# The attention output is turned by VectorE in 32x32 blocks instead of by TensorE, and the PSUM ring is laid out anew

## The reference

```python
# layer 0: softmax attention, 16 heads of 32
xn = layer_norm(x);  q, k, v = xn @ Wq + bq, xn @ Wk + bk, (xn @ Wv + bv) * mask
y  = softmax(q @ k.T + mask_bias, axis=keys) @ v            # per head
h  = layer_norm(y) * (1 + scale(emb)) + shift(emb)
x1 = x + silu(h) @ W_out0 + b_out0
# layer 1: linear attention, 8 heads of 64
xn = layer_norm(x1); q = softmax(xn @ Wq1 + bq1, axis=head features)
k  = softmax(xn @ Wk1 + bk1 + mask_bias, axis=positions);  v = (xn @ Wv1 + bv1) * mask
y  = q @ (k.T @ v)                                          # per head
out = x1 + silu(layer_norm(y) * (1 + scale) + shift) @ W_out1 + b_out1
```

## Time and profile before

| what | value |
|---|---|
| median of 3 runs | 2692.48 us (2691.06 to 2693.92) |
| profiled execution | 2693.01 us |
| its span, first to last instruction | 2691.2 us |
| mean granted TensorE clock | 0.992 |
| busy: TensorE, VectorE, ScalarE, GpSimd | 2629.1, 1793.8, 1250.1, 1348.6 us |
| first instruction of the second phase's turns | 1475.5 us into the span |

### The profile page before, as it was taken

One profiled execution on the slowest core, in us unless ns is written; L12 is line 12 of the kernel. 1 busy time (PEld: TensorE's weight loads), 2 busy tenths in 40 slices (PEclk: granted clock), 3 DMA queues, 4 the chain that ended last, 5 costly groups with the idle time before them and its releaser, 6 DMA issues. The chain is left out here.

```text
span 2691.2 us, 44011 instructions
## 1 busy us (share of the span) xinstructions
PE 2629.1 (98%) x13890; PEld 1938.4 (72%) x13890; DVE 1793.8 (67%) x3213; ACT 1250.1 (46%) x2097; POOL 1348.6 (50%) x634
## 2 busy tenths in 40 slices
PE   7999999999999999999998899999999999999999
PEld 5666666666666666666663688888888888888887
DVE  6666666666666666666664876776666776766765
ACT  3555555555565555555554333323333333333233
POOL 1666666666666666666662234334443333344343
PEclk9999999999999999999998899999999999999999
DMA  6666666666566665666674301111111111011110
GB/s 146 99 86 106 101 100 85 106 100 100 85 102 99 99 99 84 104 101 100 85 138 151 127 28 42 45 47 51 51 51 51 51 47 42 33 51 35 49 33 32
DMA packets 114916, 211.44 MB, mean 79 GB/s; under 512 B 12409, under 2 KB 14509, under 8 KB 114877
## 3 DMA queue, kind: packets, MB, share of 16 engines
q1 hardware_dynamic: 78012, 143.81, 22.9%
q10 hardware_dynamic: 36864, 67.13, 18.9%
HBM read 74.87 MB, written 34.18 MB: 41 GB/s over the span
## 5 line engine op out<-in xcount | busy, mean ns | idle before, releaser
L942 DVE TENSOR_REDUCE negmax<-max_bank 128x1 f32<-128x512 f32 x1024 | 681.8, 688 | 259.5 <-PE max_bank L535 256.6
L806 ACT ACTIVATE probs<-exp_bank 128x512 f32<-128x512 f32 x1024 | 586.9, 597 | 496.9 <-PE exp_bank L550 424.2
L297 POOL TENSOR_TENSOR probs_sum<-probs_sum,probs 128x2048 f32<-128x2048 f32 x124 | 571.6, 4610 | 31.1 <-ACT probs L806 24.4
L297 POOL TENSOR_TENSOR probs_sum<-probs 128x2048 f32<-128x2048 f32 x63 | 289.2, 4590 | 501.3 <-ACT probs L806 501.3
L550 PE MATMUL exp_bank<-q_stack,k_stack 100*128 100x512 f32 x1024 | 422.7, 422 | 2.9 <-ACT probs L806 2.0
L535 PE MATMUL max_bank<-k_stack,q_stack 98*128 98x512 f32 x1024 | 417.2, 408 | 4.7 <-DMA k_stack<-k_stage 2.3
L550 PEld LDWEIGHTS exp_bank<-q_stack,k_stack 100*128 100x128 f32 x1024 | 193.2, 189 | 127.9 <-ACT probs L806 45.8
L535 PEld LDWEIGHTS max_bank<-k_stack,q_stack 98*128 98x128 f32 x1024 | 192.8, 189 | 106.9 <-issue 54.3
L1601 POOL TENSOR_TENSOR sT_lo<-silu,sT_hi 128x512 fp32r<-128x512 f32 x124 | 167.6, 1371 | 173.2 <-DVE sT_hi L1719 173.2
L561 PE MATMUL y_bank<-probs,v_sb 128*32 128x512 f32 x2048 | 248.7, 604 | 0.0
L1346 PE MATMUL b_work<-ident,area 128*128 128x128 f32 x1536 | 190.7, 278 | 16.7 <-DVE area L1687 9.9
(11 more groups left out here) (209 smaller groups left out, 5329.3 us busy)
## 6 DMA issues: line engine op xcount, KB each, us to landing
q_stack<-q_stage ACTq DMA_DIRECT2D x128, 256.0 KB
k_stack<-k_stage ACTq DMA_DIRECT2D x128, 256.0 KB
x_sb<-in_x SPq DMA_DIRECT2D x16, 1024.0 KB, 5.3
q_stack<-q_stage SPq DMA_DIRECT2D x64, 256.0 KB
k_stack<-k_stage SPq DMA_DIRECT2D x64, 256.0 KB
yT_scratch<-y_stage SPq DMA_DIRECT2D x64, 256.0 KB
area<-yT_scratch SPq DMA_DIRECT2D x16, 1024.0 KB, 5.2
area<-in_x SPq DMA_DIRECT2D x64, 256.0 KB, 2.8
```

The lines of the kernel that those rows point to most:

```text
L297: eng.tensor_tensor(probs_sum[:, :, :], so_far, probs[:, mt, :, :], ALU.add).then_inc(probs_added, 1)
L806: act.activation(probs[:, mt, j, :], exp_bank[k % 2][:, :], ACT.Exp).then_inc(exp_done, 1)
L942: dve.tensor_reduce(negmax[:, m:m + 1], max_bank[m % 2][:, :], AXX, ALU.max, negate=True).then_inc(max_done, 1)
```

## The change

1. A is no longer done by TensorE. Its tiles leave the ring. VectorE turns each of its four tiles in 32x32 blocks from SBUF to SBUF (`turn_blocks`), then multiplies it by the reciprocals in place (`scale_heads`), then takes its statistics. TensorE still turns the sums (four small transposes).
2. So that 32x32 blocks are enough, the scratch has another layout: `store_y` writes 128 partitions x 4 runs of 512 B instead of 128 runs of 2 KB, ScalarE's `copy_y` permutes as it copies, and `load_y` is four DMAs of 32 partitions (256 KB each) instead of one of 1 MB. SyncE issues it when A's four block turns and the turn of the sums are done.
3. The four places that A leaves in the ring stay empty (`"-"`): two behind K's tiles and two between M and S. A place that nobody fills passes its wait on to the next tile in that bank.

```diff
-        ORDER = (tiles_of("KL") + [("V", 0), ("V", 1)] + tiles_of("A") + [("V", 2), ("V", 3)] + tiles_of("MSH")
+        ORDER = (tiles_of("K") + [("-", 0), ("-", 1)] + tiles_of("LVM") + [("-", 2), ("-", 3)] + tiles_of("SH")
                  + [("Q", 0), ("Q", 1)] + tiles_of("C") + [("Q", 2), ("Q", 3)] + tiles_of("JXY"))
...
-                sp.dma_start(yT_dram[b].rearrange("(j g l) t -> g j l t", j=HG, g=NG)[g], y_stage[:, g % 2, :]).then_inc(y_stored[g % 2], DMA)
+                sp.dma_start(yT_dram[b].rearrange("q j l g r -> g (j l) q r")[g],
+                             y_stage[:, g % 2, :].rearrange("p (q r) -> p q r", q=BLOCKS)).then_inc(y_stored[g % 2], DMA)
...
-                act.activation(y_stage[:, g % 2, :], y_bank[:, :], ACT.Copy).then_inc(y_read, 1)
+                act.activation(y_stage[:, g % 2, :].rearrange("p (q t a) -> p q t a", q=BLOCKS, t=TT),
+                               y_bank[:, :].rearrange("p (t q a) -> p q t a", t=TT, q=BLOCKS), ACT.Copy).then_inc(y_read, 1)
...
-                sp.dma_start(yT_sb, yT_dram[b].rearrange("(g p) t -> p g t", p=P)).then_inc(y_in, DMA)
-                sp.dma_start(sums_sb[:, :], sums_dram[b]).then_inc(y_in, DMA)
+                for q in range(BLOCKS):
+                    at = slice(q * BLOCK, (q + 1) * BLOCK)
+                    sp.dma_start(y_blocks[at, :].rearrange("l (j r) -> l j r", j=HG), yT_dram[b][q].rearrange("j l g r -> l j (g r)")
+                                 ).then_inc(y_in, DMA)
+                sp.dma_start(sums_sb[:, :], sums_dram[b]).then_inc(sums_in, DMA)
...
-                        sp.wait_ge(work_full, use(kind, b, "A", TT - 1)[1] + 1)
+                        sp.wait_ge(y_turned, TT * (b + 2))
+                        sp.wait_ge(sums_turned, b + 2)
                         load_y(b + 2)
...
-                V(kind, b, (0, 1))
+                V(kind, b, (0,))
+                if kind != "last":
+                    await_sums(b + 1)
+                V(kind, b, (1,))
...
-                    A(kind, b, b + 1)
+                    turn_sums()
                 V(kind, b, (2, 3))
```

More of the change, by code:

```diff
@@ L17 @@
+from collections import namedtuple
 from contextlib import ExitStack
@@ L1195, in order_of @@
         def order_of(kind):
+            if kind == "start":
+                return START
             if kind in ("last", "end"):
@@ L1198, in order_of, with counts @@
             return [u for u in ORDER if not (kind == "first" and u[0] in "LM")]
-        PER_ROW = len(ORDER)
-        assert PER_ROW % RING == 0
-        def use(kind, b, what, tile):
-            if kind == "start":
[L1206 to L1210, removed]
+        assert len(ORDER) % RING == 0
+        FIRST_AT = len(START)
+        ROW_AT = FIRST_AT + len(order_of("first")) - len(ORDER)
+        def counts(kind, at, tiles):
+            banks, full = [0] * RING, 0
+            for i, u in enumerate(order_of(kind)[:tiles]):
+                if u[0] != "-":
+                    banks[(at + i) % RING] += 1
+                    full += 1
+            return banks, full
+        START_READS, START_FULL = counts("start", 0, len(START))
+        FIRST_READS, FIRST_FULL = counts("first", FIRST_AT, len(ORDER))
+        ROW_READS, ROW_FULL = counts("mid", ROW_AT, len(ORDER))
+        Use = namedtuple("Use", "bank full reads")
+        def use(kind, b, what, tile):
+            order = order_of(kind)
+            n = order.index((f"end {what}" if kind == "end" else what, tile))
+            at = {"start": 0, "first": FIRST_AT}.get(kind, ROW_AT)
+            banks, full = counts(kind, at, n)
+            i = (at + n) % RING
+            if kind == "start":
+                return Use(i, full, banks[i])
+            full, reads = full + START_FULL, banks[i] + START_READS[i]
+            if kind == "first":
+                return Use(i, full, reads)
+            return Use(i, ROW_FULL * b + full + FIRST_FULL - ROW_FULL, ROW_READS[i] * b + reads + FIRST_READS[i] - ROW_READS[i])
         def bank(u):
-            return work_bank[u[0] % RING][:, :]
-        def reads(b, u):
-            return (PER_ROW // RING) * b + u[0] // RING
+            return work_bank[u.bank][:, :]
         def wait_read(eng, kind, b, what, tile):
             u = use(kind, b, what, tile)
-            eng.wait_ge(bank_read[u[0] % RING], reads(b, u) + 1)
+            eng.wait_ge(bank_read[u.bank], u.reads + 1)
         def wait_x1T(eng, kind, b):
@@ L1269, in _ @@
             load_weight("out1", out1_w)
-            sp.wait_ge(work_full, use("start", 0, "A", TT - 1)[1] + 1)
+            sp.wait_ge(y_turned, TT)
+            sp.wait_ge(sums_turned, 1)
             load_y(1)
@@ L1310, in take @@
                 u = use(kind, b, what, tile)
-                if u[0] >= RING:
-                    pe.wait_ge(bank_read[u[0] % RING], reads(b, u))
+                if not (type(u.reads) is int and u.reads == 0):
+                    pe.wait_ge(bank_read[u.bank], u.reads)
                 return bank(u)
@@ L1347, in turn, with await_sums, turn_sums @@
                 last.then_inc(work_full, 1)
-            def A(kind, b, row):
-                pe.wait_ge(y_in, 2 * DMA * (row + 1))
+            def await_sums(row):
+                pe.wait_ge(sums_in, DMA * (row + 1))
                 if not (type(row) is int and row == 0):
                     pe.wait_ge(rinv0_done, row)
[L1354 to L1360, removed]
+            def turn_sums():
+                for nt in range(TT):
+                    last = pe.transpose(sums_bank[:, nt * H0:(nt + 1) * H0], sums_sb[:, nt * P:(nt + 1) * P],
+                                        ident[0:H0, 0:H0])
+                last.then_inc(sums_turned, 1)
             def S(kind, b, row):
@@ L1456, in bias_product @@
                 last.then_inc(bias_made, 1)
-            A("start", 0, 0)
+            await_sums(0)
+            turn_sums()
             pe.wait_ge(rinv0_done, 1)
@@ L1533, in silus @@
                     u = use(kind, b, what, kt)
-                    act.wait_ge(work_full, u[1] + 1)
+                    act.wait_ge(work_full, u.full + 1)
                     if kt == 0 and kind != "start":
```

42 lines of the change are left out of this document (31 added, 11 removed).

## The result

The kernel after took 2734.98 us (median of 4 runs, 2733.71 to 2737.25), the kernel before beside it 2693.2 (4 runs, 2691.06 to 2695.04). The ratio is 1.0154 (95% interval 1.0142 to 1.0166): slower by 1.5%. The forecast was 2725.0, the range 2706 to 2746. The measured time lies above the band of the likeliest case (2719 to 2732) and nearer to rival 4's 2738. The profiled execution took 2737.25, its span is 2735.5 at a mean granted clock of 0.981 (before 2691.2 and 0.992).

What follows compares the result with a forecast made beforehand. TensorE, busy 98%, was taken as the bound, with a chain through VectorE, SyncE and GpSimd only 0.3 us from it at C. 14 x (1.7 + 0.45) + 2.3 + 0.5 = 32.9 us, so 2725 us; range 2706 to 2746.

Steps and rivals of the forecast that it cites:

- the likeliest case: Mid iterations: VectorE's longer A delays the chain to C, with the clock lost in some iterations; 2719 to 2732, chance 0.40.
- rival 4: Clock falls in every mid iteration and stays down into C, or y's load delays store 0; 2738 us, chance 0.13.
- TensorE's gain of 2.69 us per iteration: TensorE in each mid iteration: 2.05 us of turns and 0.64 us of two waits go away, so S starts earlier.
- A grows by 2.3 us from four turns at 0.60: VectorE's A: four added block turns cost 2.4 us, 0.1 is saved; growth 2.3 us (1.8 to 4.1).
- The chain's +1.7 us at C: GpSimd's low halves of S's silu, which C needs, come at 1927.5 against 1925.80: +1.7 us per mid iteration.
- The gap at Q1: TensorE between Q0 and Q1: waits 3.9 us for the silu that reads S3's place.
- The clock, 0.45 us per iteration: At Q1 after the gap: half rate would lose 0.8 to 0.9 us; half taken, 0.45 per iteration (0 to 0.9).
- The first iteration and the start, 2.8 us: First iteration: A's growth counts whole, 2.3 us, since TensorE already waits for A; before it, 0.5 us.
- Slack: Chain at C: 0.3 us of slack plus 0.37 us of a cast's wait; break-even at 0.6 us of A's growth.
- Nothing for the ring, the load of y and the attention phase: Empty ring places, y's four DMAs and the stores' shorter runs: 0 us each; upper bounds 1 per iteration (loads), 5 (attention).
- Rival 1: The change pays: TensorE stays the bound, as A grows by less than the chain's slack; 2658 us, chance 0.09.
- Rival 5: VectorE's block turns cost the upper bound of 1.06 us, A grows by 4.1 us; 2752 us, chance 0.07.

Runs made afterwards that it cites:

- Experiment 1: Kernel after, with GpSimd making the low halves of S's silu ahead of all four result biases: 2660.73 us, ratio 0.9874 against the kernel before.
- experiment 4: Kernel before, with four more unused statistics of 0.60 us each in VectorE's A: 2722.99 us, ratio 1.0106.
- 6: Kernel after, with SyncE issuing all four stores of M's tiles before any load of x: 2690.29 us, ratio 0.9988 against the kernel before.
- 7: Kernel after, with the mid iterations' block turns moved ahead of the cast of L's last silu tile: 2689.29 us, ratio 0.9983 against the kernel before.
- experiment 5: Kernel after, with 14 unused 128x512 matmuls between Q0 and Q1 of each mid iteration: 2718.56 us, ratio 1.0092 against the kernel before.
- experiment 2: Kernel before, with GpSimd making the low halves of S's silu ahead of all four result biases: 2693.08 us, ratio 0.9997.
- experiment 10: Kernel before, with one more statistics operation of 0.60 us in VectorE's A: 2700.62 us, ratio 1.0031.
- experiment 3: Kernel after, with the four empty ring places put back where A's tiles were, between V1 and V2: 2728.91 us, ratio 1.0128 against the kernel before.

## Why the prediction was right, step by step

- **TensorE's gain of 2.69 us per iteration, given back.** Right. S came 2.58 us earlier and Q1 waited. Experiment 1 frees the gain: period 71.2.
- **A grows by 2.3 us from four turns at 0.60.** Right: 2.13, at about 0.60 each. The turn in fp32 is 0.69 us as listed.
- **The chain's +1.7 us at C.** Right: +1.59 in the three iterations that kept the clock, +1.77 in experiment 4. Its links are shown one by one: the bias ahead of the low halves (experiment 1), the store behind the load of x (6), A's length (7). The gap at Q1, forecast at 3.9 us (the terms of that sum give 3.8), is 1939.53 - 1935.88 = 3.65. The lower bound of 0.48 was not VectorE's cheapest full tile, since the late cast took 0.43; nothing hung on it.
- **The clock, 0.45 us per iteration.** This is the term that was mis-sized. It measured 1.1 (2.69 - 1.59), and 1.2 by experiment 5. Both of its factors were too small. I gave the fall a chance of one half; it came in 11 of 14. And I took 0.8 to 0.9 us lost for a fall, from 1.4 at Q1; at Q1 it was 4.34 - 2.73 = 1.6 in the iteration shown, and 2.5 in the three where the lower level lasted through Q1, and the period grew by about 1.1 and 1.9 beyond the 75.4 with the clock held. In that, the kernel after is nearly rival 4 (the clock falls nearly everywhere, and in three iterations stays down until C); that the range held is owed to its having taken rival 4 in. The Trainium skill (TensorE: Matmul & The Clock Gate, Why this matters for your kernels) advises to keep TensorE fed, since a long gap brings half rate; the trace agrees for 11 of the 14 waits of 3.3 to 4.0 us, with 4.34 us in place of 2.73 in the one shown, and experiment 5 shows that unused matmuls are cheaper than the gap.
- **The first iteration and the start, 2.8 us.** Mis-sized: 6.3 up to the first Q0. VectorE's first V addition comes 1536.19 - 1533.44 = 2.75 us later, where I took 0.5: of these, 1.5 are there when K begins (1516.88 against 1515.38), 1.4 of them since the weights of K land later (1482.81 against 1481.38). The other 1.2 come from K's first six matmuls, which take 2.66 us instead of 1.44 at the lower clock (0.57 from 1516 to 1520, where it was 1.00 before). A's growth adds 2.2, as forecast, so S starts 1551.59 - 1546.63 = 4.96 later. Then S and H take 6.35 us instead of 5.03, 1.3 more, since the lower level now lasts through both. I had added A's growth to the wait and left out the clock behind it. The length of the wait alone does not decide that either: in experiment 2 the same wait is 3.88 us instead of 6.69, and S and H take 6.40. What these falls cost is read from the rows; no experiment took them away by themselves.

```profile
1551.59 6.35 PE L1379 MATMUL b_work<-ident,area 128*128 128x128 f32 x32 [10.89 <-DVE area L1727]
```

```profile
1516.00:1520.00 4.00, 4.00 (x15) 3.28 (x14) 3.95 (x7) 2.87 (x5) 0.00 (x0) 0.57 0.02 6
```

- **Slack.** 0.3 us at C was right; 0.3 + 0.37 = 0.6 as the break-even was a little high: experiment 10 lost 0.30 us per iteration with 0.60 added. The two are not simply additive, and a chain that is just late also costs a restart.
- **Nothing for the ring, the load of y and the attention phase.** Right within 1 us against the kernel before: S0 to S3 and L2, L3 show no wait. (The old places would have been 6 us better, as experiment 3 shows; I had not looked at where a ring puts the wait.) The four DMAs of y land 4.5 us after issue and delay no store (`bias_result` 0 starts 1931.05 - 1928.74 = 2.31 us after the end of M0's addition, 2.29 before). The barrier ends at 1470.24 instead of 1469.52, but in the eight profiled kernels with the new stores it ends between 1467.4 and 1470.2, in the four with the old ones between 1469.4 and 1470.0. So the 64 stores with runs of 512 B cost nothing that shows, although each lands 6.4 us after its issue (median), and the 0.7 of this pair, which is in the 6.3 above, is no effect of the change that these runs could tell from chance.

Sum with measured terms: 14 x (1.6 + 1.1) + 6.3 + 0.4 = 44.5, within 0.2 of the spans' 44.3. By the medians the kernels differ by 2734.98 - 2693.2 = 41.8 us, since the profiled execution of after was the slowest of its four. The forecast's 32.9 was short by 14 x 0.65 = 9 for the clock, 3.5 at the start and 0.4 behind it, and over by 14 x 0.1 = 1.5 for the chain. Rival 1 (the change pays) fell because its condition, a chain with slack left at C, was not met; experiment 1 meets it and gives 2661, beside the rival's 2658. Rival 5's dear turns are excluded by their 0.69 us.

## What to carry to other kernels

Moving work from the busiest engine to an idle one pays only if the idle time lies where the work lands: follow the chain through every engine's list to the point where it rejoins, and compare its slack there with the growth. When a chain passes through an engine that waits for a DMA (here GpSimd's biases behind a store), put the work that others wait for ahead of the work that waits. If a gap of TensorE can't be closed, count more than its length, since the matmuls behind it may run at half rate.

## What the runs showed of the hardware

- Waits of TensorE of 2.54 or 2.55 us lost the clock in 11 of 14 iterations (experiment 3), waits of 3.3 to 4.0 us also in 11 of 14 (after), waits of 1.0 to 1.7 us in none of 42 (experiments 4, 6 and 7). That the shorter of the first two loses it as often I had not expected. With the wait the same to 0.01 us the clock fell in one iteration and held in another; what decides, these runs do not show.
- After the fall, the 12 matmuls of Q1 took 4.34 us instead of 2.73 in the iteration shown (half rate until about 1942.7). In three of the 11 all of them ran at half rate, 5.2 us. The fall need not come within the wait: in two of the 11 it came 1.3 and 1.5 us after Q1 had begun, and in experiment 3 in six of 11 it came 0.3 to 1.1 us after V2 had begun.
- VectorE's 32x32 block turn of a 128x512 fp32 tile takes 0.69 us, 0.62 us to the next operation: like a product of the same size.
